# The sampling stage of a deformable convolution: a new instruction order on VectorE and ScalarE, with a third buffer for the interpolation factors

## The reference, cut to what matters

```python
px = gx + dx + off[..., 0]
py = gy + dy + off[..., 1]
x0 = jnp.floor(pxf)
y0 = jnp.floor(pyf)
for cx, cy in ((x0, y0), (x0 + 1, y0), (x0, y0 + 1), (x0 + 1, y0 + 1)):
    wgt = (1 - jnp.abs(pxf - cx)) * (1 - jnp.abs(pyf - cy))
    ...
    acc = acc + (wgt * valid)[..., None] * v
out = (acc * mf).reshape(B, H * W, K, G, GC).sum(axis=2)
```

## Time and profile before

| what | value |
|---|---|
| median of 3 runs | 3303.75 us (3300.03 to 3310.21) |
| the profiled execution's own time | 3312.84 us |
| its span in the profile | 3311.1 us |
| VectorE's first and last sampling add | 467.4 and 1395.3 us from the span's start |
| busy over the whole span | PE 2324.2, DVE 2259.6, ACT 1623.9, POOL 1042.6 us |

### The profile page before, as it was taken

One profiled execution on the slowest core, in us unless ns is written; L12 is line 12 of the kernel. 1 busy time (PEld: TensorE's weight loads), 2 busy tenths in 40 slices (PEclk: granted clock), 3 DMA queues, 4 the chain that ended last, 5 costly groups with the idle time before them and its releaser, 6 DMA issues. The chain is left out here.

```text
span 3311.1 us, 46654 instructions
## 1 busy us (share of the span) xinstructions
PE 2324.2 (70%) x15979; PEld 1541.9 (47%) x15979; DVE 2259.6 (68%) x4743; ACT 1623.9 (49%) x3184; POOL 1042.6 (31%) x1059
## 2 busy tenths in 40 slices
PE   5999605555655646625748999999999994502997
PEld 3555305454645645513423445445445544501775
DVE  3888658788788788637966777776776755500676
ACT  1444326666656565413437764664675641201664
POOL 0455402212122122126951122122122122174455
PEclk9999857777777767757768999999999995555998
DMA  6477848547536533283340000100100003012231
GB/s 174 103 181 164 185 136 216 183 101 193 146 96 180 154 99 97 59 264 116 94 108 1 1 1 26 33 1 26 34 1 26 14 1 105 6 40 92 73 101 51
DMA packets 343236, 304.59 MB, mean 92 GB/s; under 512 B 73775, under 2 KB 299703, under 8 KB 341536
## 3 DMA queue, kind: packets, MB, share of 16 engines
q1 hardware_dynamic: 334208, 294.00, 32.5%
q0 software_dynamic: 8800, 7.70, 0.7%
HBM read 158.50 MB, written 156.80 MB: 95 GB/s over the span
## 5 line engine op out<-in xcount | busy, mean ns | idle before, releaser
L1885 ACT ACTIVATE attn_prob<-attn_ps_e,attn_nm 128x448 f32<-128x448 f32 (+1 forms) x700 | 438.7, 632 | 333.8 <-DVE attn_nm L1972 331.0
L1789 PE MATMUL attn_ps_r<-attn_prob,attn_xs 128*128 128x448 f32 (+1 forms) x1400 | 592.8, 554 | 5.0 <-POOL attn_xs L1691 5.0
L933 PE MATMUL deform_ps_w<-all_ident,deform_grid 128*126 128x128 f32 x1568 | 295.9, 366 | 386.6 <-ACT deform_wt L902 221.3
L933 PEld LDWEIGHTS deform_ps_w<-all_ident,deform_grid 128*126 128x126 f32 x1568 | 260.4, 192 | 419.5 <-ACT deform_wt L902 234.4
L866 POOL MEMSET deform_grid<- 128x3752 f32 (+1 forms) x64 | 186.4, 2914 | 798.7 <-PE deform_ps_w L933 751.8
L1972 DVE TENSOR_REDUCE attn_nm<-attn_ps_e 128x1 f32<-128x448 f32 (+1 forms) x700 | 407.9, 615 | 38.7 <-PE attn_ps_e L1777 36.7
L1688 POOL TENSOR_TENSOR attn_xs<-attn_xa,attn_wz 128x381 f32<-128x381 f32 (+1 forms) x200 | 184.4, 947 | 722.5 <-DVE attn_wz L1993 722.5
L1016 DVE TENSOR_TENSOR deform_grid<-deform_grid,deform_prod 128x448 f32 (+1 forms) x512 | 296.9, 580 | 114.2 <-DVE deform_grid L1016 84.6
L1789 PEld LDWEIGHTS attn_ps_r<-attn_prob,attn_xs 128*128 128x128 f32 (+1 forms) x1400 | 264.5, 193 | 209.8 <-issue 178.4
L887 ACT ACTIVATE deform_hat<-deform_rel,block_negr 128x504 f32<-128x504 f32 (+1 forms) x256 | 244.1, 1123 | 203.5 <-DVE deform_rel L978 203.5
L902 ACT ACTIVATE deform_wt<-deform_ps_w 126x896 f32<-126x896 f32 x224 | 198.1, 917 | 211.2 <-PE deform_ps_o L950 107.7
(11 more groups left out here) (321 smaller groups left out, 4126.0 us busy)
## 6 DMA issues: line engine op xcount, KB each, us to landing
deform_xw<-shifted SPq DMA_DIRECT2D x112, 504.0 KB
shifted<-deform_xm SPq DMA_DIRECT2D x8, 4032.0 KB, 12.4
offsets_masks<-offs_om SPq DMA_DIRECT2D x48, 378.0 KB
deform_om<-offsets_masks SPq DMA_DIRECT2D x48, 378.0 KB, 4.1
dispatched<-rows_zero SPq DMA_DIRECT2D x1, 16512.0 KB, 49.0
experts_bi<-dispatched SPq DMA_DIRECT2D x32, 516.0 KB, 3.4
deform_xa<-projected SPq DMA_DIRECT2D x64, 168.0 KB
projected<-offs_zero SPq DMA_DIRECT2D x13, 680.0 KB
```

The lines of the kernel that those rows point to most:

```text
L933: mm = pe.transpose(ps_w[n % 2][0:NPOS, q * LANES:(q + 1) * LANES], grid[:, u % 2, at:at + NPOS], ident[:, :])
L1789: mm = pe.matmul(ps_r[n % 2][:, 0:BK], xs[0:rows, at + i, j, :], prob[0:rows, at + i, j * BK:(j + 1) * BK], start=(i == 0), stop=(i == len ...
L1885: nc.scalar.activation(prob[0:rows, slab(S) + i, ch * BK:(ch + 1) * BK], ps_e[u % NE][0:rows, 0:BK], ACT.Exp, bias=nm[0:rows, S % 2, i, ch ...
```

## The change

VectorE works two units ahead with the positions (`relative(u + 2)`) and one with the mask, the first half of the products and tap 0. Instructions that don't depend on the last add are put between the adds. The products are made in four parts of two taps (TAPS = 2, PARTS = 4) in two alternating buffers, the mask is multiplied in in two parts (taps 0 to 4, 5 to 8). The gather steps stand behind adds 5 to 8 and behind `first(u + 1)`, at positions 1 and 3. The hats have three buffers (NHAT = 3), and ScalarE makes those of unit `u + 2`: one ACTIVATE between the two halves of a subset's `keep`, the other three and the Relu behind them, and the second subset's `keep` after these. The sums have one buffer for the quad at hand; its load follows the store of the quad before at `r == 3`.

```diff
-TAPS = 4
+TAPS = 2
+PARTS = (K - 1) // TAPS
+NHAT = 3
+MASKED = (0, 5, K)
...
             def load_sums(quad):
-                if quad >= 2:
-                    sp.wait_ge(yt_st[quad % 2], 16)
-                sp.dma_start(yt[:, quad % 2, :], yt_d[quad * 128:(quad + 1) * 128, :]).then_inc(yt_in[quad % 2], 16)
+                if quad:
+                    sp.wait_ge(yt_st, 16 * quad)
+                sp.dma_start(yt[:, :], yt_d[quad * 128:(quad + 1) * 128, :]).then_inc(yt_in, 16)
 
             def store_sums(quad):
                 sp.wait_ge(sum_ok, NSTEP * NSUB * (quad + 1))
-                sp.dma_start(yt_d[quad * 128:(quad + 1) * 128, :], yt[:, quad % 2, :]).then_inc(yt_st[quad % 2], 16)
+                sp.dma_start(yt_d[quad * 128:(quad + 1) * 128, :], yt[:, :]).then_inc(yt_st, 16)
...
-                    load_sums(1)
...
-                if quad and r == 4:
+                if quad and r == 3:
                     store_sums(quad - 1)
-                if quad and r == 6 and quad + 1 < NQD:
-                    load_sums(quad + 1)
+                    load_sums(quad)
...
+            def distance(u, r):
+                act.wait_ge(rel_ok, u + 1)
+                if u >= NHAT:
+                    act.wait_ge(prod_ok, PARTS * (u - NHAT + 1))
+                nc.scalar.activation(hat_of(u)[:, :, :, r], rel_of(u), ACT.Abs, bias=tb["negr"][:, r:r + 1], scale=1.0)\
+                    .then_inc(abs_ok, 1)
+
             def hats(u):
-                act.wait_ge(rel_ok, u + 1)
-                if u >= 2:
-                    act.wait_ge(add_ok, (K - 1) * (u - 1))
-                h = hat_of(u)
+                act.wait_ge(abs_ok, R * (u + 1))
+                flat = hat[:, u % NHAT, 0:2 * K * px_of(u) * R]
+                nc.scalar.activation(flat, flat, ACT.Relu, bias=1.0, scale=-1.0).then_inc(hats_ok, 1)
+
+            def keep(u, i, h):
+                quad, subs, _, gi = unit_of(u)
+                n = turns_before(u) + 2 * i + h
+                act.wait_ge(turned, n + 1)
+                before = slab_before(quad * NSUB + subs[i])
+                if before is not None:
+                    act.wait_ge(win_ok, NXB * (before + 1))
+                nc.scalar.activation(wt[0:NPOS, i, gi, h * HALF:(h + 1) * HALF, :].rearrange("p q l -> p (q l)"),
+                                     ps_w[n % 2][0:NPOS, 0:HALF * LANES], ACT.Copy).then_inc(wt_ok, 1)
+
+            for v in range(2):
                 for r in range(R):
-                    last = nc.scalar.activation(h[:, :, :, r], rel_of(u), ACT.Abs, bias=tb["negr"][:, r:r + 1], scale=1.0)
-                last.then_inc(abs_ok, 1)
-                act.wait_ge(abs_ok, u + 1)
-                flat = hat[:, u % 2, 0:2 * K * px_of(u) * R]
-                nc.scalar.activation(flat, flat, ACT.Relu, bias=1.0, scale=-1.0).then_inc(hats_ok, 1)
-
-            def keep(u):
-                quad, subs, _, gi = unit_of(u)
-                for i, j in enumerate(subs):
-                    for h in range(2):
-                        n = turns_before(u) + 2 * i + h
-                        act.wait_ge(turned, n + 1)
-                        before = slab_before(quad * NSUB + j)
-                        if before is not None:
-                            act.wait_ge(win_ok, NXB * (before + 1))
-                        nc.scalar.activation(wt[0:NPOS, i, gi, h * HALF:(h + 1) * HALF, :].rearrange("p q l -> p (q l)"),
-                                             ps_w[n % 2][0:NPOS, 0:HALF * LANES], ACT.Copy).then_inc(wt_ok, 1)
-
-            hats(0)
-            mix(0)
-            hats(1)
-            mix(1)
-            for u in range(NU):
-                if 2 <= u + 1 < NU:
-                    hats(u + 1)
+                    distance(v, r)
+                hats(v)
+                mix(v)
+            for u in range(NU + 1):
                 if u:
-                    keep(u - 1)
-                quad, r = divmod(u, NPH * GQ)
+                    keep(u - 1, 0, 0)
+                if u + 2 < NU:
+                    distance(u + 2, 0)
+                if u:
+                    keep(u - 1, 0, 1)
+                if u + 2 < NU:
+                    for r in range(1, R):
+                        distance(u + 2, r)
+                    hats(u + 2)
+                if u and len(unit_of(u - 1)[1]) > 1:
+                    keep(u - 1, 1, 0)
+                    keep(u - 1, 1, 1)
                 if u < 2:
                     mix(2 + u)
+                quad, r = divmod(u, NPH * GQ)
                 if quad + 1 < NQD and r in (4, 6, 8, 10):
                     mix(4 * quad + r // 2 + 2)
-            keep(NU - 1)
...
             def products(u, part):
-                dve.wait_ge(masked, u + 1)
-                if part or u:
-                    dve.wait_ge(add_ok, (K - 1) * u + TAPS * part)
-                n = TAPS * px_of(u)
-                nc.vector.tensor_tensor(prod[:, 0:n, :, :], columns(u, 1 + TAPS * part, TAPS), rows(u, 1 + TAPS * part, TAPS),
-                                        ALU.mult).then_inc(prod_ok, 1)
+                n, place = TAPS * px_of(u), u * PARTS + part
+                dve.wait_ge(masked, 2 * u + (1 if TAPS * (part + 1) < MASKED[1] else 2))
+                if place >= 2:
+                    dve.wait_ge(add_ok, TAPS * (place - 1))
+                nc.vector.tensor_tensor(prod[:, place % 2, 0:n, :, :], columns(u, 1 + TAPS * part, TAPS),
+                                        rows(u, 1 + TAPS * part, TAPS), ALU.mult).then_inc(prod_ok, 1)
 
             def first(u):
-                dve.wait_ge(masked, u + 1)
+                dve.wait_ge(masked, 2 * u + 1)
                 dve.wait_ge(blank, u + 1)
-                nc.vector.tensor_tensor(region(u, 0), columns(u, 0, 1), rows(u, 0, 1), ALU.mult)\
-                    .then_inc(first_ok, 1)
+                nc.vector.tensor_tensor(region(u, 0), columns(u, 0, 1), rows(u, 0, 1), ALU.mult).then_inc(first_ok, 1)
 
             def add(u, tap):
                 place = region(u, tap)
                 n = px_of(u)
-                dve.wait_ge(first_ok, u + 1)
-                dve.wait_ge(prod_ok, 2 * u + 1 + (tap - 1) // TAPS)
-                if tap > 1:
+                part, i = divmod(tap - 1, TAPS)
+                if i == 0:
+                    dve.wait_ge(prod_ok, u * PARTS + part + 1)
+                if tap == 1:
+                    dve.wait_ge(first_ok, u + 1)
+                else:
                     dve.wait_ge(add_ok, (K - 1) * u + tap - 1)
-                i = (tap - 1) % TAPS
-                nc.vector.tensor_tensor(place, place, prod[:, i * n:(i + 1) * n, :, :], ALU.add).then_inc(add_ok, 1)
+                nc.vector.tensor_tensor(place, place, prod[:, part % 2, i * n:(i + 1) * n, :, :], ALU.add).then_inc(add_ok, 1)
...
+            def summed_in(u):
+                quad, r = divmod(u, NPH * GQ)
+                phase, pos = divmod(r, GQ)
+                if u < GQ or pos not in (1, 3):
+                    return None
+                before, phase = (quad, phase - 1) if phase else (quad - 1, NPH - 1)
+                return before * NSUB + PHASES[phase][pos // 2] if pos // 2 < len(PHASES[phase]) else None
+
             relative(0)
-            waiting, late = [], []
+            relative(1)
+            mask_rows(0, 0)
+            mask_rows(0, 1)
+            products(0, 0)
+            first(0)
+            products(0, 1)
             for u in range(NU):
-                if u + 1 < NU:
-                    relative(u + 1)
-                mask_rows(u)
-                products(u, 0)
-                first(u)
+                w, more = summed_in(u), u + 1 < NU
                 for tap in range(1, K):
-                    if tap == 1 + TAPS:
-                        products(u, 1)
                     add(u, tap)
-                    if tap >= K - NSTEP and late:
-                        gather(late[0], tap - (K - NSTEP))
-                if late:
-                    late.pop(0)
-                late, waiting = late + waiting, []
-                quad, subs, _, gi = unit_of(u)
-                if gi == GQ - 1:
-                    waiting = [quad * NSUB + j for j in subs]
-            for w in waiting:
+                    if tap == 1 and u + 2 < NU:
+                        relative(u + 2)
+                    elif tap == 2 and more:
+                        mask_rows(u + 1, 0)
+                    elif tap == 3:
+                        products(u, 2)
+                    elif tap == 4 and more:
+                        mask_rows(u + 1, 1)
+                    elif tap == 5:
+                        products(u, 3)
+                    if w is not None and tap >= K - GQ:
+                        gather(w, tap - (K - GQ))
+                    if tap == 7 and more:
+                        products(u + 1, 0)
+                if more:
+                    first(u + 1)
+                if w is not None:
+                    gather(w, GQ)
+                if more:
```

(43 more changed lines are left out.)

## The result

| | before | after |
|---|---|---|
| median | 3304.84 us (4 runs) | 3214.99 us (4 runs, 3209.91 to 3217.28) |
| ratio to before | | 0.971, 95% interval 0.9685 to 0.9736 |
| profiled execution, its span | 3312.84, 3311.1 us | 3216.21, 3214.5 us |
| first relative to last sum of the stage (starts) | 456.3 to 1411.3: 955.0 us | 457.5 to 1321.7: 864.2 us |

The kernel became faster by 90 us; forecast were 99 us, 3205 us. The gain is where it was placed: of the 96.6 us between the two profiled spans the sampling stage has 90.8. The other 5.8 us lie outside it, where the two kernels are the same, and are no part of the gain.

A forecast was written before the change was run, and what follows sets the result against it. VectorE was taken to bound the sampling stage, largely by adds waiting on adds. Quad 0 gains 21.6 us and quads 1 to 3 77.1, together 98.7: 3214 from the profiled 3312.84, or 3205 us against the median; range 3165 to 3260.

The forecast's parts named there:

- Chain and unit: VectorE's clean full unit: independent work between adds leaves one chained pair, and the unit falls from 13.70 to 11.5 us.
- Rival (c): VectorE's adds: independence saves nothing, all stay at 0.86 us, and the kernel takes 3335 us; chance 0.04.
- Ring: Transposes, ScalarE's copies and ACTIVATE, clearing, tap 0: cleared grid ready at 10.7 us, wanted at 11.5; slack 0.8, cost 0.
- rival (a): The ring of engines binds: 1 us more per full unit, 2 more per stall, 3277 us; chance 0.18.
- the walk: Step-by-step timing through TensorE, ScalarE and the clearing to tap 0, in a clean unit and at phase changes.
- Phase changes: Tap 0 waiting for a cleared grid: 6.6 us twice a quad, 5.5 at the half phase; 18.7 a quad against 12.5.
- Rival (b): The phase-change stalls vanish because the copies come early enough: 4 x 18.7 us back, 3130 us; chance 0.07.
- SyncE at cost 0: Loads of offsets keep about 18 us of lead where 25 stood, the longest landing is 12.6; cost 0.
- the first two units gain nothing: Start of quad 0: relative(3) waits for the same load, tap 0 of unit 2 comes at about 503 us, as before.
- The half phase and the 5 us for contention: Half phase 37.2 us against 44.6; 5 us a quad given back because durations were clean ones, making -30.7 into -25.7.
- Sums: Single buffer of sums: SyncE waits 7.4 us for a store with loads of offsets behind it; cost 0.
- Register loads: Nine a unit at 0.30 us, 2.7 us in all, covered by the instruction ahead within 11.5 us; cost 0.

The follow-up runs named there:

- e1: Changed kernel with VectorE's adds in pairs: work behind adds 1, 3, 5 and 7 moved behind adds 2, 4 and 6; 3235.88 us, ratio to before 0.9783.
- e5: Changed kernel with four buffers of offsets and masks instead of three, the fourth loaded at the start; 3195.61 us, ratio to before 0.9686.
- e2: Changed kernel with ScalarE's old order: all ACTIVATEs and the Relu of unit u + 2 ahead of the copies of unit u - 1; 3383.0 us.
- e7: Changed kernel with two buffers of hats instead of three; 3342.53 us.
- e4: Changed kernel with the first window's gather steps behind adds 2 to 6 at position 1 of phases 1 and 2; 3188.37 us, ratio to before 0.9655.
- e8: Kernel before with only one buffer of sums, loaded behind the store of the quad before at r == 4; 3309.3 us, ratio 1.0011.

## Why the prediction was right

**Chain and unit.** Right: 11.35 us against the 11.5 forecast. e1, with the same instructions, loses 21 us to waits and lost overlap: what it has more of is chained adds, 203 against 41. Independent neighbours start 0.53 us apart, ahead of the 0.62 us that an add takes. Rival (c) is out.

**Ring.** It did not bind, so rival (a) is out. In the unit shown above TensorE's last half transpose and GpSimd's clearing are

```profile
739.78 0.98 PE L940 MATMUL deform_ps_w<-all_ident,deform_grid 128*126 128x128 f32 x7 [1.08 <-ACT deform_wt L900]
...
740.83 3.22 POOL L866 MEMSET deform_grid<- 128x3752 f32 x1 [8.14 <-PE deform_ps_w L940]
```

The clearing ends at 744.05, and tap 0 comes at 745.86: 1.8 us, where the walk had 1.3 (10.2 to 11.5, of which it gave 0.5 to a register load). The walk is right up to this half transpose, which starts 5.3 us behind tap 0 as worked out; it took 0.98 us, at a granted clock of 1.00 (737.9 to 740.8 us), where the walk had 1.63, half of the 3.25 of the earlier trace rows, measured at 0.50. So part of the slack is luck: in a clean unit of e5 with the clock at 0.50 throughout that half transpose took 1.75 us and the slack is 1.1 us (the clearing ends at 1134.14, tap 0 starts at 1135.20). That the ring is near is what e2 and e7 show: 16 to 17 us a unit as soon as hats or their buffer lengthen it.

**Phase changes.** Right: stalls of 5.9 to 6.2 us in full units (6.6 forecast; the prediction's own walk, start at 18.3 and VectorE at 12.0, gives 6.3) and 4.4 to 5.2 at the half phase (5.5). Rival (b) is out. The walk took 0.86 us for a half transpose, half of the 1.72 of the earlier trace rows; behind the sampling shown above the first two took 1.72 us and the last 0.98. The slower ones of its upper bound are the 1.63 of the earlier trace rows; the stalls stayed 2.4 us under that bound of 8.6. e4 shows that the fourth gather step starts the count.

**Quad by quad**, from tap 0 of one quad to that of the next (the last: to the last add): gains of 11.3, 27.4, 30.3 and 20.8 us (241.4, 232.4, 234.9 and 220.0 before, 230.1, 204.9, 204.6 and 199.2 after), where 21.6 and three times 25.7 were forecast. Two terms were mis-sized:

- *SyncE at cost 0, and "the first two units gain nothing".* The step was right for unit 1 (tap 0 of unit 2 at 504.17, forecast 503) and wrong for unit 3. Waits for offsets were among the prediction's own signs of being wrong, and this one came; what it upsets is this term, not the rest of the sum. SyncE and VectorE, kernel after:

```profile
517.69 4.69 SPq L819 DMA_DIRECT2D deform_xw<-shifted  x4
522.43 2.07 SPq L788 DMA_DIRECT2D deform_om<-offsets_masks  x1
...
530.47 1.12 DVE L985 TENSOR_TENSOR deform_rel<-deform_om,block_nsk 128x504 f32<-128x504 f32 x1 [12.46 <-DMA deform_om<-offsets_masks]
```

  The load for unit 5 stands behind the first windows, which wait for the mixed pixels to land (SyncE's wait for it is 11.4 us, once). In the kernel before it was issued at nearly the same time, but VectorE needed it later, and found it there:

```profile
520.31 2.08 SPq L785 DMA_DIRECT2D deform_om<-offsets_masks  x1
...
529.25 1.17 DVE L978 TENSOR_TENSOR deform_rel<-deform_om,block_nsk 128x504 f32<-128x504 f32 x1
```

  These 12.5 us are more than the 10.3 by which quad 0 fell short, and e5 takes them back. The lead of 18 us that the prediction gave holds for a SyncE that isn't held up; behind unit 4 (0.9 us) no offsets came late.
- *The half phase and the 5 us for contention.* From tap 0 to tap 0 the phases of quad 1 took 49.0, 57.4, 55.9 and 42.7 us; the clean sum had 48.7, 57.9, 57.9 and 37.2. Some 2 us of this only moved: the last units of a phase make the positions, the mask and the products of the next one's first units, so the third phase has lighter work, that of half units, and the half phase heavier work, that of full ones. The sum left this out. Besides, VectorE waited in the half phase 2.2 us for hats of the next quad's full unit, 1.1 for one more cleared grid and 0.6 for a sampled window, while the stall was 0.9 shorter than forecast:

```profile
867.48 0.41 DVE L1013 TENSOR_TENSOR deform_grid<-deform_hat 128x224 f32 x1 [1.14 <-POOL deform_grid L866]
...
894.40 0.74 DVE L993 TENSOR_TENSOR deform_hat<-deform_hat,deform_om 128x560 f32<-128x560 f32 x1 [2.18 <-ACT deform_hat L891]
```

  The quad took 204.9 us where the clean sum was 201.7. The 5 us that were given back for contention covered this, but for another reason than the one named: that was luck.

Quad 3 gained less: before it had been 12 to 15 us shorter than quads 1 and 2, after only 5. The prediction took the three for alike; why quad 3 was shorter was not looked into.

**Sums.** Cost 0 was right: e8 has it with the store at r == 4; in the kernel after, with the store at r == 3, SyncE waited for stores 21.4 us in three times, and no load of offsets came late there.

**Register loads.** Cost 0 was right, and they may have given a gain that the prediction did not name. Loads of over 0.6 us, mostly 0.9, are as frequent as before (61 of 576 against 63). Before, 45 chained adds waited more than 0.4 us each, 28.5 us in all, and ahead of 39 of them stood such a load: six from 814 to 821 us took 0.88 to 0.96, and the adds there came 1.2 us apart. After, no chained add waits that long: with an independent instruction between two adds the long loads are hidden as well. How much of the 28.5 us these loads cost was not tested apart.

## What to carry to other kernels

A wait between dependent instructions, and the overlap that goes with it (0.24 and 0.09 us an add in the earlier trace rows, 81.2 and 59.8 us in this stage), is worth removing when the engine is the bound and independent work can stand between: price it from a place in the trace where such work already stands there. Before counting the gain, walk the ring of buffers through the other engines: an engine with slack by its sum (ScalarE, 9.5 of 11.4 us) can still set the pace by its order, and undoing its part of the change cost more than the whole gain (e2: 168 us against 90). Check the lead of each load where its queue is held up, at the start above all, not only in the steady state.

## What was not expected

TensorE's granted clock in the clean unit was 0.50 before and 0.80 after, though it had the same 28 transposes in the unit. Inside the unit it was 0.51 up to 737.9 us, while TensorE transposed without a break, and 1.00 from there to 740.8, where the last two half transposes took 1.0 us instead of 1.6. It looks as if units 11.4 us apart instead of 13.7 raised the clock, but the runs speak against that. The same unit of quad 3 in e5 takes 11.36 us too, at 0.50 throughout:

```profile
1123.80:1135.20 11.40, 6.17 (x28) 5.36 (x26) 11.15 (x16) 9.01 (x9) 3.23 (x1) 0.50 0.71 258
```

In the kernel before, that unit of quad 2 had 0.62 at 14.0 us. What raises the clock stays open.

And a chained add cost less in the new order: in e1 it starts 0.76 us (the median) after the add that it waits for, in the kernel after 0.82 in the unit shown, against 0.86 in the earlier trace rows. The adds before had three waits each, that of the kernel after has two, those of e1 one; whether these make the difference was not tried apart.
